# Message stages of a graph network: TensorE takes two tiles at a time, sums them four tiles later, and fetches and border stores are moved

## What is computed

```python
def _gine_layer(x, src, dst, edge_attr, eps, We, be, W1, b1, gamma, beta, W2, b2):
    e = edge_attr @ We + be
    m = jax.nn.relu(x[src] + e)                                        # message of each edge
    agg = jax.ops.segment_sum(m, dst, num_segments=x.shape[0])         # sum of the messages of a node
    h = ((1.0 + eps) * x + agg) @ W1 + b1
    ...
    return jax.nn.relu(h @ W2 + b2)
```

## Time and profile before

| | |
|---|---|
| median of three runs | 4528.63 us |
| profiled execution | 4494.73 us, its span 4492.9 us (1.8 us lie around it) |
| TensorE (PE) busy | 4033.5 us, 90% of the span |
| VectorE (DVE), ScalarE (ACT), GpSimd (POOL) busy | 62%, 46%, 34% |
| mean granted TensorE clock | 0.924 |
| first to last TensorE work of stages 2, 3, 4 | 2526.39 to 2599.98, 3129.25 to 3193.00, 3716.85 to 3788.24 us |

### The profile page before, as it was taken

How to read it: one execution, slowest core, us unless ns; L and a number is a source line. 1 busy time by engine, 2 the same in 40 slices (tenths; PEclk the granted TensorE clock), 3 DMA queues, 4 the chain that set the end, 5 groups by cost and what they waited for, 6 DMA issues and landing times. The chain is left out here.

```text
span 4492.9 us, 64635 instructions
## 1 busy us (share of the span) xinstructions
PE 4033.5 (90%) x22551; PEld 3277.7 (73%) x22551; DVE 2779.0 (62%) x5334; ACT 2048.8 (46%) x3496; POOL 1549.0 (34%) x1483
## 2 busy tenths in 40 slices
PE   7887899898978768789999989999899998999977
PEld 3447788777767446549988579986699874998855
DVE  5665656578977677567854455543555444556878
ACT  1222223232338434265567533475433764334556
POOL 1442266217850758644400323101332004330033
PEclk9998999999989678799999999999999998999965
DMA  8995488539976869864423555324754237444678
GB/s 307 400 344 178 152 265 282 184 124 338 390 279 197 318 159 176 159 225 153 158 81 114 198 180 163 103 96 150 233 162 125 84 118 245 158 158 129 184 196 248
DMA packets 462324, 888.88 MB, mean 198 GB/s; under 512 B 71189, under 2 KB 112966, under 8 KB 461248
## 3 DMA queue, kind: packets, MB, share of 16 engines
q1 hardware_dynamic: 294682, 521.98, 34.1%
q0 software_dynamic: 90016, 237.51, 19.1%
q10 hardware_dynamic: 77338, 125.65, 7.9%
HBM read 609.74 MB, written 303.62 MB: 203 GB/s over the span
## 5 line engine op out<-in xcount | busy, mean ns | idle before, releaser
L2178 POOL DMA_INDIRECT hidden_agg<-edge_sums,edge_where x316 | 354.2, 1121 | 713.4 <-DVE layer_raw_inner L2265 287.7
L2011 POOL DMA_INDIRECT message_x<-g,edge_partner x120 | 114.5, 955 | 754.9 <-POOLq L150 458.3
L783 PE MATMUL hidden_O<-hidden_xh,layer_hi_inner 128*128 128x256 f32 (+1 forms) x1280 | 366.4, 286 | 0.0
L785 PE MATMUL hidden_O<-hidden_xl,layer_hi_inner 128*128 128x256 f32 (+1 forms) x1280 | 360.3, 281 | 0.0
L784 PE MATMUL hidden_O<-hidden_xh,layer_lo_inner 128*128 128x256 f32 (+1 forms) x1280 | 359.6, 281 | 0.0
L2222 ACT ACTIVATE hT_inner<-hidden_O,hidden_b 128x256 f32<-128x256 f32 (+1 forms) x320 | 124.2, 471 | 330.1 <-PE hidden_O L785 324.6
L783 PE MATMUL root_O<-root_hi,root_xh 128*128 128x512 f32 (+1 forms) x632 | 254.7, 403 | 15.3 <-DVE root_xl L1183 11.3
L783 PE MATMUL output_O<-layer_hi_inner,output_hh 128*128 128x512 f32 (+1 forms) x632 | 250.2, 396 | 0.4 <-DVE output_hl L2359 0.4
L785 PE MATMUL output_O<-layer_lo_inner,output_hh 128*128 128x512 f32 (+1 forms) x632 | 249.7, 395 | 0.0
L784 PE MATMUL output_O<-layer_hi_inner,output_hl 128*128 128x512 f32 (+1 forms) x632 | 249.6, 395 | 0.0
L2368 DVE TENSOR_TENSOR layer_raw_inner<-output_O,output_b2t 128x1024 f32<-128x1024 f32 x80 | 96.9, 1211 | 246.2 <-PE output_O L785 246.2
(11 more groups left out here) (501 smaller groups left out, 12564.3 us busy)
## 6 DMA issues: line engine op xcount, KB each, us to landing
edge_sums<-message_res SPq DMA_DIRECT2D x160, 256.0 KB, 2.4
layer_raw_inner<-g SPq DMA_DIRECT2D x78, 512.0 KB
g<-layer_raw_inner SPq DMA_DIRECT2D x78, 512.0 KB
room<-in_L_gnn_basis SPq DMA_DIRECT2D x30, 1280.0 KB
order_basis<-in_L_gnn_basis SPq DMA_DIRECT2D x18, 1280.0 KB
edge_sums<-relation_res SPq DMA_DIRECT2D x82, 256.0 KB
order_x<-in_x SPq DMA_DIRECT2D x39, 512.0 KB
normed<-order_y ACTq DMA_DIRECT2D x39, 512.0 KB
```

The costliest lines, as they stand in the source:

```text
L783: eng.matmul(out, a_hi, b_hi, start=start, stop=False)
L785: return eng.matmul(out, a_hi, b_lo, start=False, stop=stop)
L2011: eng.indirect_dma_start(x[t % R][:, :], None, table, bass.IndirectOffsetOnAxis(ap=ed.partner[1][:, t:t + 1], axis=0)).then_inc(ga[t % R], 16)
L2178: eng.indirect_dma_start(agg[j % R][0:n, :], None, ed.sums[1], bass.IndirectOffsetOnAxis(ap=ed.where[1][0:n, c:c + 1], axis=0)).then_inc(g ...
```

## The change

Five edits, four of them for stages 2 to 4 alone.

- TensorE's list is written by `pair(p)`: two tiles a = 2p and b = 2p + 1 at a time. All its waits stand ahead of the first product: for `ml` of tile b - 4, for `z` of tile b - 4, for `res` of tile b - 7, and for the gather of tile a. Then come the edge term and identity product of a, the edge term of b, and the four selection products of tiles a - 4 and b - 4, with no wait among them.
- ScalarE copies B out with a lag of 4 iterations in place of 3.
- The weight is fetched in iteration 8 of ScalarE in place of 0, and split from tile 12 on in place of 6.
- In all four stages SyncE stores the borders of the last four tiles first and their sums behind them.
- In all four stages 16 more products with the identity stand between the last selection product and the wait of line 2131.

```diff
--- before.py
+++ after.py
@@ -1937,7 +1937,8 @@
     CHUNK = 5
     HEAD = XR * P
     LOOK = 3
-    SPLIT_AT, ROWS_AT = 24 if normal else 6, 34 if normal else 22
+    SPLIT_AT, ROWS_AT, FETCH_AT = (24, 34, 12) if normal else (12, 22, 8)
+    LAST_FEW = 4
     batches = MESSAGE_BATCHES
     of = lambda b: slice(batches[b].start, batches[b].stop)
     closes = lambda t: t + 1 == ET or BATCH_OF[t + 1] != BATCH_OF[t]
@@ -1987,16 +1988,26 @@
                         eng.dma_start(select[:, ts, :].bitcast(F32), ed.select[:, ts, :]).then_inc(s[f"sel{c}"], 16)
                 eng.wait_ge(s["zero"], 1)
 
+                def store_border(t):
+                    eng.wait_ge(s["res"], t + 1)
+                    eng.dma_start(borders[t:LAST + t + 1:LAST, :], res[t % Q][0:P:P - 1, :]).then_inc(st[t % Q] if t < ET - Q else s["edge"], 16)
+
+                def store_sums(t):
+                    eng.dma_start(ed.sums[1][t * P:(t + 1) * P, :], res[t % Q][:, :]).then_inc(st[t % Q] if t < ET - Q else s["tail"], 16)
+
                 def store(t):
-                    main, border = (st[t % Q], st[t % Q]) if t < ET - Q else (s["tail"], s["edge"])
-                    eng.wait_ge(s["res"], t + 1)
-                    eng.dma_start(borders[t:LAST + t + 1:LAST, :], res[t % Q][0:P:P - 1, :]).then_inc(border, 16)
-                    eng.dma_start(ed.sums[1][t * P:(t + 1) * P, :], res[t % Q][:, :]).then_inc(main, 16)
+                    store_border(t)
+                    store_sums(t)
                     if t == ROWS_AT:
                         eng.wait_ge(s["wlo"], KC)
                         for g in range(2):
                             eng.dma_start(raw[:, g * TILES:(g + 1) * TILES, :], rows(table, g, False)).then_inc(s["xin"], 16)
-                static_pipeline([(0, store)], ET)
+                for t in range(ET - LAST_FEW):
+                    store(t)
+                for t in range(ET - LAST_FEW, ET):
+                    store_border(t)
+                for t in range(ET - LAST_FEW, ET):
+                    store_sums(t)
                 eng.wait_ge(s["hres"], 1)
                 eng.dma_start(ed.sums[1][EP:EP + ET, :], hres[:, :]).then_inc(s["done"], 16)
                 eng.wait_ge(s["tail"], 16 * Q)
@@ -2091,9 +2102,9 @@
                         eng.wait_ge(ga[2], 16)
                         split.load(eng)
                 if normal:
-                    static_pipeline([(0, norm), (1, high), (4, result), (2, weight_high), (SPLIT_AT - 12, fetch)], ET)
+                    static_pipeline([(0, norm), (1, high), (4, result), (2, weight_high), (FETCH_AT, fetch)], ET)
                 else:
-                    static_pipeline([(0, fetch), (0, high), (3, result), (2, weight_high)], ET)
+                    static_pipeline([(FETCH_AT, fetch), (0, high), (4, result), (2, weight_high)], ET)
 
             @block.tensor
             def _(eng):
@@ -2126,7 +2137,29 @@
                 keep_awake(eng, H[:, 0:P], ident, 18 if ahead else 34)
                 if not ahead:
                     eng.wait_ge(s["terms"], 32)
-                static_pipeline([(0, attr), (2, sums)], ET)
+
+                def pair(p):
+                    a, b = 2 * p, 2 * p + 1
+                    if a >= XR:
+                        eng.wait_ge(s["ml"], b - XR + 1)
+                    if XR <= b < ET:
+                        eng.wait_ge(s["z"], of_dve(b - XR))
+                    wait(eng, s["res"], b - XR - 2)
+                    if b < ET:
+                        eng.wait_ge(ga[a % R], (a // R + 1) * 16)
+                        eng.matmul(X[a % XR][:, :], edge_terms[:, a * P:(a + 1) * P], attr_terms[:, :], start=True, stop=False)
+                        eng.matmul(X[a % XR][:, :], ident[:, :], x[a % R][:, :], start=False, stop=True).then_inc(s["X"], 1)
+                        eng.matmul(X[b % XR][:, :], edge_terms[:, b * P:(b + 1) * P], attr_terms[:, :], start=True, stop=True).then_inc(s["E"], 1)
+                    if a >= XR:
+                        for t in (a - XR, b - XR):
+                            eng.matmul(B[t % 3][:, :], select[:, t, :], mh[t % W][:, :], start=True, stop=False)
+                            eng.matmul(B[t % 3][:, :], select[:, t, :], ml[t % W][:, :], start=False, stop=True).then_inc(s["B"], 1)
+                if normal:
+                    static_pipeline([(0, attr), (2, sums)], ET)
+                else:
+                    for p in range((ET + XR) // 2):
+                        pair(p)
+                keep_awake(eng, X[0][:, 0:P], ident, 16)
                 eng.wait_ge(s["edge"], 16 * Q)
                 eng.matmul(H[:, :], ed.merge[1][:, :], borders[:, :], start=True, stop=True).then_inc(s["H"], 1)
```

## The result

The changed kernel takes 4621.06 us (median of 4 runs, 4614.93 to 4635.81), the kernel before 4526.46 beside it. The profiled execution took 4619.76 us with a span of 4618.0, 125 us above that of before. The forecast was 4500.5 us.

What follows compares the result with a forecast made beforehand. TensorE was taken as bound by waits in each two tiles (some 2.5 us of work in 3.04), plus standstills with low clock. 26.1 + 2.0 = 28.1 us off 4494.7 gave 4466.6, plus 34: 4500.5 us, range 4487 to 4521.

Steps and rivals of the forecast that it cites:

- the later fetch: Weight fetch in stages 2 to 4, issued at T + 10.5: about half a us lost in stage 2, where now 2.
- half a us leaves the clock alone: Stages 2 to 4: the half us lost to a late gather is too short to lower TensorE's clock.
- the sum: Stages 2 to 4 gain 26.1 us with pairs at 3.00, stage ends 2.0: 28.1 us off in all.
- slower: Rival: a pair waiting for a gather also holds back earlier tiles' selection products; at 3.75 a pair, 4539 us; 6%.
- The loop through `res`: From a pair's start through its first sums and ScalarE's copy to the next pair: 2.95 us, range 2.85 to 3.05.
- the price of waiting at five places: Kernel before: of 3.04 us for two tiles TensorE has some 2.5 of work, the rest is waiting.
- The DMA bound: A pair moves 1.057 MB; at 351 GB/s, the highest rate held for 20 us, it takes 3.01 us.
- Pair 2: First pair to wait for `ml` of tile 1; starts at T + 4.1 us, T being the first edge term.
- Both remain: Rival: the standstills of stages 2 and 4 both stay; gain 28.1 - 17.5 = 10.6, 4518 us; 14%.
- the eight us that late gathers didn't explain: Stage 4, tile 6: identity product starts at 3725.49, ScalarE reads its result only at 3734.13; no row names why.
- The end of a stage: Last selection product to copy of H: H starts at 4.4, copy at 5.55; gain 0.5 x 4 = 2.0 us.
- The case of products at half clock: Stage ends: 16 new products at half clock would end at 8.6, cost 2.5 each time, 10 in all; not expected.

Runs made afterwards that it cites:

- e9: Changed kernel with a pair's waits still in front, but its products alternating: first tile, its sums, second tile, its sums; 4524.89 us, kernel before 4510.45.
- e15: The kernel of e9 timed again, against the kernel before: 4518.14 us, ratio 1.0021 [0.9999, 1.0043].
- e7: Kernel before with only the late weight fetch, the new order of the last stores and the 16 products: 4507.29 us, ratio 0.9985.
- e8: Kernel before with four accumulators for the sums in place of three, nothing else: 4516.74 us, ratio 1.0.
- e18: Kernel before with gathers at most six tiles ahead of the sum in stages 2 to 4, nothing else: 4498.72 us, ratio 0.9964.
- e4: Changed kernel with the weight fetched at tile 0 of stages 2 to 4 as before: 4615.82 us, ratio 1.0221.
- e2: Kernel before with TensorE's pairs alone, none of the other parts of the change: 4634.24 us, ratio 1.027.
- e10: Changed kernel with the order of products kept, each wait put directly ahead of the product that needs it: 4615.32 us, kernel before 4510.45.
- e14: Changed kernel's pair, waits in front, ordered both edge terms, first sums, tile product, second sums: 4519.84 us, kernel before 4507.46.

## Why the prediction was wrong

*The step that failed* is in the later fetch: "half a us leaves the clock alone", and with it that the sum prices every pair at 3.00 us and has no term for pairs at 1.2 GHz. They took 5.52: 17 x 2.52 x 3 = 129 us, which covers the loss of 117 in the three stages. In stage 2 the clock fell before the fetch was issued. In stages 3 and 4 it was down within 5 us of the first products at 3174.73 and 3805.89, behind waits of 1.21 and 0.54 us, with no long standstill (a window of stage 3, then the fall in stage 4, after):

```profile
3179.70:3184.70 5.00, 5.00 (x8) 2.15 (x8) 1.98 (x3) 0.83 (x2) 2.94 (x4) 0.50 0.71 206
3810.12 0.49 PE L2150 MATMUL message_X<-kept_attr_terms,kept_edge_terms 5*128 5x512 f32 x1 [0.54 <-issue]
3810.54 1.87 PE L2151 MATMUL message_X<-message_x,cst_ident 128*128 128x512 f32 x2
```

The identity product at 3810.54 already lasts 1.87 where it lasts 1.13 at full clock: half a us did not leave the clock alone. And in the new order of products it did not come back. The rival "slower" had a front wait as its mechanism; e9 and e15, with front waits, rule it out for a loss of more than 0.43%. The loss was in no case of mine. Why this order doesn't regain the clock stays open.

*The loop through `res`* was the right mechanism and the wrong size: 3.48, not 2.95. The mis-sized terms are edge b to the first selection product, 0.42 for 0.23, the next product 0.33 for 0.23, and copy to TensorE 0.24 for 0.05. The last was an estimate from gaps between other engines. With them 17 x 0.48 x 3 = 24 of the 28 us go, at full clock too. Behind this stands a misreading: the wider steps were put down to waits ("the price of waiting at five places"), but the 0.42 and the 0.33 stand within a pair, where nothing is waited for.

*The DMA bound*, 3.01 a pair, agrees with the pace of e7, e8 and e9, 3.01 to 3.04, but that the transfers set it is not shown. TensorE is shown without idle time in these stretches, and in e18 two tiles take 3.03 also from 3150 to 3160, at a DMA share of 0.87 and 284 GB/s; TensorE's own list explains the pace as well. *Pair 2* started at 2543.39, T + 4.23, for T + 4.1: right.

*The later fetch* gains nothing: the standstill comes ahead of it (in stage 4 the fetch is issued at 3827.0, behind a wait of 3.48 us before 3824.14), and e4 with the early fetch has it too (2.33 us before 2563.14, 5.01 before 3836.81). "Both remain", at 14%, had this right, that the standstills don't go with the fetch; the clue was in my own text, the eight us that late gathers didn't explain. e18 shows the depth of the gathers behind it; why ten in flight hold back a result whose product the records show as done isn't shown.

*The end of a stage* gained more than was forecast. Last product to copy of H is 5.0, 5.22, 5.47 and 5.33 us in stages 1 to 4 after, for 6.3, 6.04, 6.04 and 7.15 before: 4.5 us together, for 2.0 forecast. (Both parts of the change at this place stand in all four stages, so three of the five edits, not four, are for stages 2 to 4 alone.) Stage 2 after, 2654.97 - 2649.75 = 5.22:

```profile
2649.75 0.63 PE L2156 MATMUL message_B<-message_ml,kept_select 128*128 128x512 f32 x1
2650.18 3.77 PE L791 MATMUL message_X<-cst_ident 128*128 128x128 f32 x32
2653.88 1.05 PE L2164 MATMUL message_H<-message_borders,edge_merge 105*40 105x512 f32 x2
2654.97 0.68 DVE L2076 COPY message_hres<-message_H 40x512 f32<-40x512 f32 x1 [7.50 <-PE message_H L2164]
```

In stages 2 to 4 the clock came back some half a us or less behind the start of the 16 products, that is behind the twelve sums in a row, after 100 us of pairs in which it had not. That these products are needed for it is not so: e2 has it back without them. But there it was lost again in a wait of 3.24 us, and H took 1.93 in stage 3; here H ran in 1.05 where it took 1.93 before. The case of products at half clock, "cost 2.5 each time", left out H itself: 8.6 + 1.12 - 6.04 = 3.7.

## What to carry over

Regrouping a list of products changes more than its waits: price every step of the new loop from a row with the same neighbour, and ask what the loop costs if a wait leaves TensorE at 1.2 GHz, for it may stay there. In this kernel the list that alternates the edge and identity products with the sums came back to 2.4 GHz, and the one that blocks four sums did not. Look at the granted clock by window, since the busy time did not tell the two apart. A deep prefetch can cost more at the start of a stage than it hides: six gathers ahead were better than ten, by 0.4%.

## What was unexpected in the hardware

At 0.50, TensorE busy 20.00 of 20 us stayed at 1.2 GHz (e10), while with 21.98 busy of 30 it kept 2.4 GHz (e14). The Trainium skill, "TensorE: Matmul & The Clock Gate", section "What's actually happening", says that activity releases the throttle; this trace does not agree where activity is read as the busy time of the profile. The Trainium skill, on the same page, section "Seeing it yourself", warns that clock records may be unreliable; here the durations of the products, 0.63 for 0.40 us, agree with the records. What the chip counts stays open.
